# A fused RWKV-and-experts kernel on one core: the program's beginning in another order, and its end without one drain

## The reference

```python
x = x + attention(layernorm(x), ...)      # x: 4 batches x 1024 tokens x 256 channels, f32
x = x + experts(layernorm(x), ...)        # 8 experts, top 2, capacity 1.25, 896 hidden

def attention(x, ...):                    # RWKV, 16 heads of 16 channels
    xx = shift_by_one_token(x) - x
    xk, xv, xr, xg = (x + xx * maa for maa in (maa_k, maa_v, maa_r, maa_g))
    r, k, v, g = xr @ Wr.T, xk @ Wk.T, xv @ Wv.T, gelu(xg @ Wg.T)
    w = exp(-exp(time_decay)); u = time_faaaa            # one number a head
    Wmat = where(i > j, w ** (i - j - 1), 0) + eye(Q) * u
    # chunk by chunk: y = (r @ k) * Wmat @ v + r @ state * w**q
    #                 state = w**Q * state + (k * w**(Q-1-q)) @ v
    return (groupnorm(y) * ln_w + ln_b) * g @ Wo.T
```

## Time and profile before

| what | value |
|---|---|
| median of three runs | 855.15 us (853.99 to 855.53) |
| the profiled execution | 854.25 us, of which its span is 852.2 us |
| TensorE busy | 812.1 us, 95% of the span |
| VectorE, ScalarE, GpSimd busy | 499.1, 490.7, 462.0 us (59, 58, 54%) |
| last chain | TensorE 27% of the span, then GpSimd's last transfer |

### The profile page before, as it was taken

The page is one execution under the profiler, slowest core; times in us unless marked ns, Lnnn a source line. Parts: engine busy times, 40 slices in busy tenths (PEclk is TensorE's granted clock), DMA queues, the critical chain, the costliest instruction groups (busy, mean ns, idle before and its releaser), DMA issues. The chain is left out here.

```text
span 852.2 us, 17481 instructions
## 1 busy us (share of the span) xinstructions
PE 812.1 (95%) x6343; PEld 677.2 (79%) x6343; DVE 499.1 (59%) x1237; ACT 490.7 (58%) x876; POOL 462.0 (54%) x497
## 2 busy tenths in 40 slices
PE   3999999999999998999999999999999999999995
PEld 2678887777788776787997788997788898888884
DVE  6888888899888767343542443543543544443441
ACT  4578888888888787354643543643543543552431
POOL 6454476777787756475434355434356443436214
PEclk9999999999999999999999999999999999999998
DMA  5852132113111122654334145333334342404113
GB/s 149 342 196 70 34 117 74 52 52 96 42 50 65 53 78 75 208 157 82 101 67 91 59 106 94 100 68 40 109 95 72 92 110 28 121 2 51 20 14 42
DMA packets 50474, 74.05 MB, mean 87 GB/s; under 512 B 5056, under 2 KB 42176, under 8 KB 50368
## 3 DMA queue, kind: packets, MB, share of 16 engines
q1 hardware_dynamic: 35488, 53.46, 19.1%
q0 software_dynamic: 14592, 19.18, 13.5%
q10 hardware_dynamic: 288, 0.01, 0.0%
HBM read 38.41 MB, written 34.22 MB: 85 GB/s over the span
## 5 line engine op out<-in xcount | busy, mean ns | idle before, releaser
L1592 POOL DMA_INDIRECT out<-ysb,index x80 | 124.7, 1559 | 145.3 <-DVE ysb L1831 111.5
L1945 PE MATMUL p<-xh,whi 128*128 128x512 f32 (+2 forms) x504 | 185.6, 368 | 6.1 <-issue 5.2
L1807 DVE TENSOR_TENSOR hid<-gated,p 128x512 f32<-128x512 f32 (+1 forms) x126 | 81.1, 643 | 181.1 <-ACT gated L1654 181.1
L1947 PE MATMUL p<-xh,wlo 128*128 128x512 f32 (+2 forms) x504 | 185.3, 368 | 0.0
L1946 PE MATMUL p<-xl,whi 128*128 128x512 f32 (+2 forms) x504 | 184.6, 366 | 0.0
L1971 PE MATMUL py<-w,hh 128*128 128x512 f32 x448 | 162.6, 403 | 3.7 <-DVE hl L1088 3.0
L1654 ACT ACTIVATE gated<-p 128x512 f32<-128x512 f32 (+1 forms) x126 | 71.0, 564 | 162.2 <-PE p L1947 162.2
L1581 POOL TENSOR_TENSOR wlo<-wraw,whi 128x448 fp32r<-128x448 f32 x56 | 70.7, 1266 | 94.7 <-ACT whi L1640 90.6
L1945 PEld LDWEIGHTS p<-xh,whi 128*128 128x128 f32 x504 | 94.7, 188 | 23.4 <-issue 8.0
L1970 PE MATMUL py<-w,hl 128*128 128x256 f32 x384 | 108.6, 283 | 0.0
L1946 PEld LDWEIGHTS p<-xl,whi 128*128 128x128 f32 x504 | 94.8, 188 | 15.3
(11 more groups left out here) (204 smaller groups left out, 1440.4 us busy)
## 6 DMA issues: line engine op xcount, KB each, us to landing
wraw<-in_w SPq DMA_DIRECT2D x24, 896.0 KB, 4.8
disp<-wraw SPq DMA_DIRECT2D x16, 662.5 KB, 9.3
xtok<-disp SPq DMA_DIRECT2D x16, 530.0 KB, 4.9
x_ring<-in_x SPq DMA_DIRECT2D x16, 256.0 KB, 3.5
out<-x SPq DMA_DIRECT2D x16, 256.0 KB, 2.2
xtok<-disp SPq DMA_DIRECT2D x8, 265.0 KB, 4.2
out<-ysb,index POOLq DMA_INDIRECT x80, 3.8
disp<-row,slot_i POOLq DMA_INDIRECT x64
```

The costliest lines, as they stand in the source:

```text
L1592: nc.gpsimd.indirect_dma_start(out, bass.IndirectOffsetOnAxis(ap=index[e.const % 2][:, t:t + 1], axis=0), ysb[j % NY][:], None, compute_op ...
L1807: nc.vector.tensor_tensor(hid[k][:, 0:w], gated[k][:, 0:w], p3[k][:, 0:w], ALU.mult).then_inc(hid_ready, 1)
L1945: nc.tensor.matmul(dst[:, 0:w], hi[m][:, wcut], xh[xcut], start=(kt == 0), stop=False)
L1947: ins = nc.tensor.matmul(dst[:, 0:w], lo[m][:, wcut], xh[xcut], start=False, stop=(kt == KT - 1))
```

## The change

It has six parts.

2. `decay_logs()` moves on VectorE from step -1, behind the mixing of the first block, to step -3, ahead of `shifted(0)`. It waits there for rstd1_ready, which GpSimd's first norm raises.
3. The second block's statistics, norm and normed tokens (`stats1(1)`, `norm1(1)`, `normed1(1)`) come later: on VectorE behind `center_v`, on GpSimd behind `empty_rows`, on ScalarE at the end of step -1. The third block's statistics move behind the first four masks.
4. `mask_table()` and `decay_tables()` on ScalarE move ahead of the copies of the first block's receptance and key.
5. The bonus takes two instructions of 128x2048 in place of the 16: `bonus()` writes the identity times u into a free stretch of kept.xtok, `add_bonus()` adds that to dmask.
6. TensorE gets 14 matmuls of the identity with itself (128x128, into pY) ahead of the first transposes, and 6 behind them. Nothing reads what they write.

```diff
--- before.py
+++ after.py
@@ -56,6 +56,7 @@
 NW = KT * F
 WPC = NW // WP
 RING = 7
+BEFORE_TURN, BEHIND_TURN = 14, 6
 ROWS = 3
 
 
@@ -202,7 +203,7 @@
             sb2, ps2 = tensors(ctx)
             split.append(Split(sb2, 1))
             second = phase_b(nc, sb2, ps2, ctx, sem, ident, split, wraw, w1, w2, w3, taken, disp, out, kept)
-            with nc.Block() as block:
+            with nc.Block(no_gpsimd_drain=True) as block:
 
                 @block.sync
                 def _(sp):
@@ -620,7 +621,10 @@
             weight_low(c - 6)
             if c >= TAIL - 2:
                 scatter(c - 3)
-            norm1(c + 3)
+            if c == -1:
+                norm1(1)
+            if c != -2:
+                norm1(c + 3)
             if c == -3:
                 tables()
             chain.reset()
@@ -809,23 +813,25 @@
             group_log(c - 1)
             value(c)
             turned1(c + 1)
+            if c == -1:
+                mask_table()
+                decay_tables()
             group_rstd(c - 1)
             gate(c)
-            normed1(c + 2)
+            if c != -1:
+                normed1(c + 2)
             scaled(c - 1)
             normed2(c - 2)
             receptance(c + 1)
             pairs(c + 1)
-            if c == -1:
-                mask_table()
             key(c + 1)
-            if c == -1:
-                decay_tables()
             square_y(c)
             turned2(c - 2)
             weight_high(c - 4)
             keep_y(c)
             column(c + 1)
+            if c == -1:
+                normed1(1)
 
         logit_exp(12)
         group_log(14)
@@ -904,13 +910,16 @@
             chain.add(nc.vector.tensor_scalar(early_end[:], base0[:], float(CHUNKS[EARLY][1] * P), None, ALU.add))
             chain.link(nc.vector.tensor_scalar(before[0][:, 0, :], base0[:], 1.0 / P, None, ALU.mult))
 
-        def bonus(half):
+        on_diagonal = kept.xtok[:].rearrange("p t c -> p (t c)")[:, 0:H * Q].rearrange("p (h q) -> p h q", q=Q)
+
+        def bonus():
             dve.wait_ge(late_in, 16 * NLATE)
+            chain.link(nc.vector.tensor_tensor(on_diagonal, ident[:].unsqueeze(1).to_broadcast([P, H, Q]),
+                                               u_sb[:].unsqueeze(2).to_broadcast([P, H, Q]), ALU.mult))
+
+        def add_bonus():
             dve.wait_ge(set_act, 2)
-            for h in range(half * H // 2, (half + 1) * H // 2):
-                ins = nc.vector.scalar_tensor_tensor(dmask[:, h, :], ident[:], u_sb[:, h:h + 1], dmask[:, h, :],
-                                                     ALU.mult, ALU.add)
-            chain.link(ins)
+            chain.link(nc.vector.tensor_tensor(dmask[:], dmask[:], on_diagonal, ALU.add))
 
         def stats1(b):
             if 0 <= b < STEPS:
@@ -1091,7 +1100,6 @@
         for c in range(-3, TAIL):
             mixing(c + 1, 1)
             if c == -1:
-                decay_logs()
                 head_parity()
             normed_y(c - 1)
             state_a(c)
@@ -1100,19 +1108,25 @@
             mask(c, 1, 2)
             mask(c, 1, 3)
             state_b(c)
-            stats1(c + 3)
+            if c not in (-2, -1):
+                stats1(c + 3)
+            if c == -3:
+
+                dve.wait_ge(rstd1_ready, 1)
+                decay_logs()
             mixing(c + 1, 2)
             if c == -1:
                 center_v()
+                stats1(1)
             residual(c - 1)
             slots(c - 3)
             logit_max(c - 2)
             stats2(c - 1)
             if c == -1:
-                bonus(0)
+                bonus()
             decayed_k(c + 1)
             if c == -1:
-                bonus(1)
+                add_bonus()
             best_two(c - 2)
             tally(c - 2)
             mask(c + 1, 0, 0)
@@ -1120,6 +1134,7 @@
             mask(c + 1, 0, 2)
             mask(c + 1, 0, 3)
             if c == -1:
+                stats1(2)
                 slot_tables()
             shifted(c + 2)
             masked_kv(c + 1)
@@ -1369,10 +1384,19 @@
                     ins = nc.tensor.matmul(dst, split.up[1][m][:, wcut], kept.xh[:, kt, early_cols], start=False, stop=(kt == KT - 1))
             ins.then_inc(h_done, 1)
 
+        def warm(n):
+
+            for _ in range(n):
+                nc.tensor.matmul(pY[:, 0, 0:P], ident[:], ident[:], start=True, stop=True)
+
         for c in range(-1, TAIL):
+            if c == -1:
+                warm(BEFORE_TURN)
             scores_a(c)
             across(c, 0)
             turn1(c + 1)
+            if c == -1:
+                warm(BEHIND_TURN)
             project_g(c)
             outer(c)
             within(c, 0, 0)
```

## The result

The changed kernel takes 849.40 us (median of 18 runs, 848.4 to 853.5 but for a single run of 2723 us), against 854.54 for the kernel before in 18 runs of the same kind: ratio 0.9944, interval 0.9932 to 0.9956, or 4.8 us less (3.8 to 5.8). The forecast was 849.6, 846.8 to 852.6. The profiled execution took 850.92 us with a span of 848.9, so 2.0 us lie outside it, as before (2.05).

The account below looks back on a forecast made before the run. Bound by VectorE's list until TensorE's steady work at 30.3 us, and by a bare DRAIN at the end. 4.6 + 0.5 = 5.1 us off the profiled 854.25 gives 849.15; half of the median's 0.9 added, 849.6, range 846.8 to 852.6.

Parts of the forecast that it names:

- The end: Behind the last transfer: GpSimd's DRAIN of 4.605 us goes, 4.6 us gained, bounds 0 and 4.6.
- the rival with 0.15: At the end: the drain is paid outside the span, only 0.5 us gained in all, 854.2; chance 0.15.
- The decay product and collisions: VectorE's start: product moved to about 7.3 nearly free, but VectorE and GpSimd shut each other out; masks at 23.6, not 25.47.
- the collision-free 21.5: Start of the first masks, in us, by VectorE's list alone, without any shut-out by GpSimd; before it was 25.47.
- The term of the collisions, 2.1: Time VectorE loses to GpSimd before the first masks: 2.1 us taken, ends 0 and 3.4.
- The late norm: Second block's norm on GpSimd, shut out by the bonus instructions, ends at 23.9; transposes start at 25.1, before at 25.04.
- The first rival: At the beginning: small collisions or norm slips through, start at 27.4 to 28.6, 2.3 us gained, 847.8; chance 0.22.
- Steady work: TensorE's second receptance projection starts at 29.8 instead of 30.30: 0.5 us gained, bounds -0.9 and +2.9.
- the added matmuls: TensorE's start: may speed the first projection by 1.5 us, but VectorE's list sets the masks, so counted as nothing.
- the 5.1 of the sum: Whole kernel: 4.6 us at the end plus 0.5 at the beginning, 5.1 us off.
- The prediction's own last sign of being wrong: Forecast is wrong if TensorE's steady stretch loses time that it did not lose before.
- The short spell at the slower pace: TensorE's pace falls in the gap before the second block's transposes: 3.0 of the 5.1 us lost, 852.6; chance 0.06.

Follow-up runs that it names:

- drain_only: The kernel before with one edit, `nc.Block(no_gpsimd_drain=True)`, so without GpSimd's DRAIN at the end; 857.85 us, ratio 0.9947.
- bonus16: The changed kernel with the bonus as 16 short 128x128 instructions again in place of two long ones; 857.24 us, ratio 0.9944.
- decay_back: The changed kernel with the decay product and ScalarE's tables back in their old places (parts 2 and 4 undone); 864.51 us, ratio 1.0018.
- after_again: The changed kernel as it is, measured once more on another chip; 849.15 us, ratio 0.9937.
- warm_wide: The changed kernel with 4 added matmuls of 512 columns in place of 20 of 128; 847.68 us, ratio 0.9924.
- no_warm_again: The changed kernel without the 20 added matmuls, measured once more on another chip; 847.05 us, ratio 0.9917.

## Why the prediction was right, point by point

**The end: right, in mechanism and size.** 4.6 us were predicted; 4.7 between the two traces, 4.6 in drain_only by itself. Outside the span lie 2.0 to 2.1 us in the runs of before and 1.7 to 2.0 in most without the DRAIN (2.8 at most), never the 6 and more of the rival with 0.15, which is refuted.

**The decay product and collisions: right in kind, too dear.** The product ran from 7.23, as said, in 2.29 us, not 2.50 (the 2.50 of the earlier trace rows had a gate mixing of GpSimd beside it that had started 0.12 us sooner), and the bonus pair took 2.26 and 2.28. With that, the collision-free 21.5 would have been some 0.7 less, and the masks stood at 22.66 where 23.6 was taken. The term of the collisions, 2.1, was mis-sized only a little against this corrected list (22.66 - 20.8 is 1.9); the durations taken from the one long instruction were the rest. It was made of other parts than listed: the centring lost 1.0 behind r_dec and the small instruction on vmean 0.6 behind the sum of the gate.

**The late norm: right.** It ended at 22.68 (predicted 23.9), the transposes came at 23.86 (25.1), shut out twice as the prediction had it. bonus16 shows the cause by taking it away. But two chains were so close that what it cost at the projection is 0.5 us of 2.75. The first rival, with small collisions or a norm that slips through, put the start at 27.4 to 28.6; the measured 28.56 lies in that range, but neither of its two reasons came true.

**Steady work: 1.74 us sooner, 0.5 predicted, inside its bounds of -0.9 to 2.9.** TensorE's side held to the distances of the kernel before: 23.86 + 3.6 would be 27.5, and the scores start at 27.48. The term was mis-sized by its start alone. Against the old beginning on drain_only's chip the gain is 2.4 us (28.58 against 30.96), so 1.74 is itself good to some 0.7 only.

**The step that failed: the added matmuls, of which the prediction says "I count nothing".** They gave 0.3 to 0.6 us and cost 1.5 to 2.1 net on the same chip, from 430 us later on, through their number. The prediction looked at what hides their time on TensorE and never at the program's length. This error and the one before it are of the same size and opposite, 1.2 us too little gained at the beginning against about 1.5 lost later, and this is why the total of 4.8 stood so near the 5.1 of the sum. The number was right in part by luck. The prediction's own last sign of being wrong, that the steady stretch would lose time that it did not lose before, is what happened.

**The short spell at the slower pace** did not come at the beginning (0.66 and 1.89 behind the transposes' wait), but it is real: decay_back shows it behind a gap of 3.95 us. The prediction saw that the clock column reads 1.00 where the durations say half pace, and gave no reason. The trace's record of the clock has its first entry at 15.0 us in the kernel before and at 7.7 in the changed one, just where the matmuls' distance halves (0.43 to 0.22 us in the projection, 0.21 to 0.11 in the added matmuls); ahead of it nothing is recorded, and the column shows 1.00 for that. The durations, by which the prediction went, are right.

**Open.** Between 500 and 632 us the profile of the changed kernel loses another 0.7 us of its lead, which the third halt accounts for. Between 720 and 764 it loses 0.3, and after_again 0.7; neither has a halt there but the branches' own. warm_wide loses 1.1 there, 0.4 of it in its own halt, while no_warm_again loses nothing. The halts at the branches themselves differ too, 1.47 to 1.91 us, and what sets their length was not tested. Why the clock falls behind the branch in two traces of fourteen can't be told from one profiled execution of each kernel.

## What to carry to other kernels

Follow a gain at the beginning to the end of the span by the starts of the same instruction in both traces: the place where the lead drops is the place of the next cause, however far from the edit. Instructions added to an engine's program can cost more than their time: they shift all later code, here against fixed places at which TensorE had to wait, very likely the borders of the blocks in which it is fetched. So where the program has branches, look for new waits "for issue" just behind them, and get the same work from fewer instructions. And before you cost a removed wait, see how many chains end near it; here shortening one by 2.75 us gave 0.5, and two at once gave 0.8 that the next block took back.

## What the runs showed of the hardware that was not expected

- A barrier's DRAIN on GpSimd behind many indirect transfers takes 4.6 us, though the transfers have landed, and nothing later asks for that time when it is left out (2.0 to 2.1 us outside the span in the runs of before, 1.7 to 2.0 in most without it).
- Behind the taken branch at the end of an expert's step TensorE halts 1.5 to 1.9 us, and 0.0 to 0.5 behind the other one (L2071), although its queue spends 3.3 to 4.0 us in either: in the changed kernel's profile the queue came to it at 606.39 with 15 matmuls of 0.23 us still to be done, which cover most of it, and to the halting one at 452.66 with 17 of 0.12 us. A further 0.9 to 1.6 us goes if it runs out of instructions seven matmuls later, and 0.2 to 1.1 at thirteen.
- In two traces of fourteen the clock fell from 2.4 to 1.2 GHz some 1.5 us behind a branch's halt (0.50 in one window of 5 us, 0.82 in the next) and stayed there for 6.8 us; with the halt that followed this cost 4 us of lead.
- GpSimd's instructions on two columns, 0.20 to 0.25 us alone, take 1.7 to 2.0 beside a VectorE instruction of 2048 columns with both inputs in SBUF; the wait ends when that one ends, no matter how small the work.
- In the first microseconds matmuls run at half pace (3.5 to 3.8 us for 1.99 us of work) while the granted clock reads 1.00, since its record begins only where the pace rises: the pace at the beginning is read from durations.
